# Moving GpSimd's stream sums and the first gating products into the convolution of a language-model tower

## The chip, the cores and the metric

The kernel runs on one core of a Trainium2 chip: TensorE (PE) for products and turns, VectorE (DVE), ScalarE (ACT) and GpSimd (POOL) for elementwise work, SyncE (SP) for most transfers. The metric is the device time of one execution in microseconds. One more execution was recorded by the hardware profiler, and its times are those of the rows below.

## The reference, cut to what matters

Four streams (b = 0 to 3) of 1024 tokens go through a tower of an embedding, four blocks with residual sums, 64 features wide. The change touches the first block only, a gated long convolution in place of attention:

```
h = take(W.T, x)                                  # embedding, masked where x == 0
xn = layernorm(h)
u = silu(xn @ u_w.T + u_b);  v = silu(xn @ v_w.T + v_b)      # 192 wide
y = irfft(rfft(v, 2n) * rfft(a, 2n))[:n]          # a: kernel of a small position network
out = (u * y) @ o_w.T + o_b
x_r = silu(srms((xn - out) @ t_w.T + t_b))
h = h + xn + x_r                                  # the block gives xn + x_r, h is the residual
xn2 = layernorm(h)                                # what the next block reads
```

After it come a product-key memory block, an attention block and a mixture of experts, which this text calls the mixer.

## The kernel before, in words

The program is four blocks one after the other, each with one hand-written list of instructions for each engine; all engines meet at a barrier between blocks: `embed_stage`, `conv_stage`, `gate_stage`, `mixer_stage`. Order within an engine is that of its list, and semaphores say what waits for what. The tensors st_h, tz_xn, tz_u, tz_v and tz_y hold h, xn, u, v and y of all four streams, 128 tokens to a row of partitions, 8 such rows to a stream.

`conv_stage` transforms v by products with a table, multiplies by the kernel's spectrum on VectorE (`product`), and transforms back: 64 products on TensorE (L576), each pair copied out by ScalarE (L598). The back transform runs in two halves: half 0 holds streams 0 and 1, half 1 streams 2 and 3. VectorE's `gather_waves(half)` sums the 16 waves of a half into tz_y. All its operands lie in SBUF.

`gate_stage` goes through the streams in a pipeline. VectorE multiplies u and y of stream 0 (L967), GpSimd those of streams 1 to 3 (`gate_rows`, L792), and GpSimd adds xn to h for each stream between them (`add_rows`, L796). On TensorE, `turn(b)` transposes u*y (16 products, L816 and L817), `project(b)` multiplies by o_w (L826, L827), `weigh(b)` by t_w (L835), `flip(b)` transposes the new xn. On ScalarE, `copy_gated(b)` copies the turned product out of PSUM (L870, L871), then `square`, `root`, `silu`, `deviation` and `copy_rows` follow. On VectorE, four memsets set the rows of ones and zeros that carry the biases (L968 to L971, semaphore ones_set), then `differ(b)` takes xn - out (L928), `mean` and `divide` normalise, `norm_a(b)` adds to h and begins the layer norm (L952 to L955), `norm_b(b)` ends it. TensorE waits for the weights and for the ones ahead of the first turn. The identity that the transposes use is loaded once in the embedding and once more in the gate.

## Time and profile before

| | us |
|---|---|
| median of 3 runs | 3322.91 (3321.53 to 3324.5) |
| the profiled execution: time | 3329.95 |
| its span | 3328.1 |
| embedding | 0 to 91 |
| convolution | 91 to 209 |
| gate | 209 to 290.6 |
| mixer | 290.6 to 3328.1 |

Over the whole span TensorE is busy 84% and VectorE 82%, but that is an average over stages. The rows of the sections below are of three kinds. A timeline row gives when an instruction (or a run of like ones) starts, how long it takes, its engine and line, and in brackets how long the engine had been idle and what released it. A table row gives a stretch and how long each engine was busy in it, with the granted TensorE clock (1.00 is 2.4 GHz, 0.50 is 1.2 GHz). An fp32 product shows as two passes in a row's count.

### The profile page before, as it was taken

What the parts mean: (1) busy time and instruction counts of PE and PEld (TensorE: products, weight loads), DVE (VectorE), ACT (ScalarE), POOL (GpSimd) and SP (SyncE); (2) the same over time, 40 slices, a digit from 0 to 9 for tenths busy, and PEclk for the clock granted to TensorE, in tenths of its full rate; (3) what the DMA queues carried; (4) which work ended last, traced back from release to release, by engine and by line L of the source; (5) the groups of instructions that cost most, each with busy time, mean ns of one, the idle gap of its engine ahead of it and who ended that gap; (6) DMA issues with size and microseconds to landing.
All of it is one profiled execution on the core that took longest, in us unless ns stands there. A gap on an engine that the chain in (4) does not pass through costs nothing. (4 is left out here: it accounts for less than half of the span.)

```text
span 3328.1 us, 39343 instructions
## 1 busy us (share of the span) xinstructions
PE 2803.7 (84%) x9750; PEld 1333.8 (40%) x9750; DVE 2745.1 (82%) x10000; ACT 2051.7 (62%) x4514; POOL 2049.2 (62%) x2094
## 2 busy tenths in 40 slices
PE   4863466888989898989897989999988889899988
PEld 2431222343434343434344434344444434444433
DVE  8666987989898989897889998997989898966423
ACT  4222455676767676767686767676686767676422
POOL 4010577777777777777666777776657777776200
PEclk8975677999999999999898989999999899999989
DMA  1001122222222222222121222221212222221000
GB/s 43 26 10 49 34 65 63 64 64 61 67 64 65 63 64 65 63 64 63 49 67 41 70 61 70 56 73 50 66 47 62 65 65 63 64 63 49 20 0 4
DMA packets 85770, 179.92 MB, mean 54 GB/s; under 512 B 40193, under 2 KB 41251, under 8 KB 85542
## 3 DMA queue, kind: packets, MB, share of 16 engines
q0 software_dynamic: 66560, 135.40, 16.0%
q1 hardware_dynamic: 18982, 42.01, 4.0%
q8 instruction: 79, 1.29, 0.2%
q14 instruction: 149, 1.22, 0.1%
HBM read 176.22 MB, written 1.05 MB: 53 GB/s over the span
## 5 line engine op out<-in xcount | busy, mean ns | idle before, releaser
L1333 POOL DMA_INDIRECT mx_G<-in_kv_table,mx_slot_i x2048 | 1993.1, 973 | 815.4 <-issue 606.4
L1361 PE MATMUL mx_acc<-mx_W,mx_table 128*128 128x512 f32 x2048 | 1114.1, 626 | 0.3 <-ACT mx_kvT L1562 0.3
L1719 DVE SCALAR_TENSOR_TENSOR mx_W<-mx_D,mx_W 128x512 f32<-128x512 f32 x1024 | 697.2, 681 | 260.6 <-ACT mx_W L1555 258.5
L1623 ACT ACTIVATE mx_GT<-mx_G,mx_slot_w 128x128 f32<-128x128 f32 x2048 | 759.0, 494 | 208.9 <-DMA mx_G<-in_kv_table,mx_slot_i 208.5
L1555 ACT ACTIVATE mx_W<-mx_D 128x512 f32<-128x512 f32 x1024 | 606.9, 593 | 165.1 <-PE mx_D L1351 160.7
L1361 PEld LDWEIGHTS mx_acc<-mx_W,mx_table 128*128 128x128 f32 x2048 | 412.6, 203 | 193.8 <-issue 114.8
L1351 PE MATMUL mx_D<-mx_U,mx_pick_b 96*128 96x512 bf16 x1024 | 412.3, 403 | 60.0 <-DVE mx_W L1719 58.4
L1579 ACT ACTIVATE mx_PT<-mx_area 128x512 f32<-128x512 f32 x480 | 246.8, 514 | 284.9 <-PE mx_area L1411 147.0
L1373 PE MATMUL mx_O<-mx_PT,mx_KVs 128*65 128x512 f32 (+3 forms) x768 | 312.7, 489 | 16.9 <-ACT mx_OT L1571 8.7
L1387 PE MATMUL mx_area<-mx_KTa,mx_QTa 64*128 64x512 f32 (+3 forms) x384 | 179.3, 548 | 156.7 <-DVE mx_mx_part L1954 126.2
L1936 DVE TENSOR_REDUCE mx_KVs<-mx_GT 128x128 f32<-128x2048 f32 x128 | 291.8, 2280 | 6.9 <-ACT mx_GT L1623 6.7
L1351 PEld LDWEIGHTS mx_D<-mx_U,mx_pick_b 96*128 96x128 bf16 x1024 | 106.4, 104 | 270.1 <-issue 133.1
L1373 PEld LDWEIGHTS mx_O<-mx_PT,mx_KVs 128*65 128x65 f32 x768 | 101.7, 137 | 216.2 <-issue 171.3
L1387 PE MATMUL mx_area<-mx_KTb,mx_QTb 64*128 64x512 f32 (+3 forms) x384 | 183.1, 559 | 0.0
L1387 PEld LDWEIGHTS mx_area<-mx_KTa,mx_QTa 64*128 64x128 f32 x384 | 59.6, 194 | 303.7 <-DVE mx_mx_part L1954 194.9
L1407 PE MATMUL mx_area<-mx_QTa,mx_KTa 65*128 65x512 f32 (+3 forms) x384 | 158.6, 494 | 3.2 <-DVE mx_mx_part L1954 2.9
L1407 PE MATMUL mx_area<-mx_QTb,mx_KTb 128*128 128x512 f32 (+3 forms) x384 | 156.2, 488 | 0.0
L1954 DVE TENSOR_REDUCE mx_mx_part<-mx_area 128x2 f32<-128x1024 f32 (+3 forms) x128 | 130.1, 1016 | 12.5 <-PE mx_area L1387 6.9
L1636 ACT ACTIVATE mx_hot<-mx_FI 128x864 uint16<-128x864 uint32 x128 | 116.7, 913 | 23.1 <-DVE mx_row L1889 23.1
L1458 PE MATMUL mx_X<-st_keys,mx_qpk 128*128 128x256 f32 x256 | 76.0, 423 | 43.0 <-ACT mx_S L1591 20.3
L792 POOL TENSOR_TENSOR tz_u<-tz_u,tz_y 128x1536 f32<-128x1536 f32 x3 | 11.8, 3950 | 160.4 <-POOLq L460 160.4
L1407 PEld LDWEIGHTS mx_area<-mx_QTa,mx_KTa 65*128 65x128 f32 x384 | 71.6, 192 | 86.2 <-issue 65.3
(380 smaller groups left out, 4370.6 us busy)
## 6 DMA issues: line engine op xcount, KB each, us to landing
mx_table<-in_kv_dense SPq DMA_DIRECT2D x64, 512.0 KB, 3.7
mx_G<-in_kv_table,mx_slot_i POOLq DMA_INDIRECT x2048
tz_table<-in_c_dft SPq DMA_DIRECT2D x1, 2048.0 KB
tz_table<-in_c_idft SPq DMA_DIRECT2D x8, 256.0 KB, 2.6
out_h<-mx_xc SPq DMA_DIRECT2D x4, 256.0 KB, 3.8
mx_G<-in_c_pick SPq DMA_DIRECT2D x1, 528.0 KB
st_h<-in_tok_W,em_ids POOLq DMA_INDIRECT x32, 2.5
st_keys<-in_pk_keys SPq DMA_DIRECT2D x1, 512.0 KB, 3.9
```

The source lines that it names most:

```text
L1333: pool.indirect_dma_start(G[g % RING][:, r, :], None, a["kv_table"], bass.IndirectOffsetOnAxis(slot_i[n % 2][:, k, r:r + 1], 0))\
L1351: pe.matmul(D_ps[c % 3][:, :], pick_b[:, step, :], U[n % 2][:, ih, cols], start=False, stop=True, skip_group_check=True).then_inc(d_ready, 1)
L1361: pe.matmul(acc[:, :], table[:, tile, :], W[c % TILE_RING][:, :], start=(tile == 0), stop=(tile == TILES - 1)).then_inc(applied, 1)
L1373: pe.matmul(O_ps[0:D + 1, first:HALF], values, PT[k % 4][:, first:HALF], start=(kb == 0), stop=last, skip_group_check=True).then_inc(weigh ...
L1387: last = pe.matmul(area[indices[x] % 2][:, 0:w], QT[x][lanes[x], qb * P:qb * P + P], KT[x][lanes[x], kh * HALF:kh * HALF + w], start=True, ...
L1407: last = pe.matmul(bank[:, first:HALF], KT[x][:, kb * P:kb * P + P], QT[x][:, group * HALF + first:(group + 1) * HALF], start=True, stop=n ...
L1555: act.activation(W[c % TILE_RING][:, :], D_ps[c % 3][:, :], ACT.Exp).then_inc(p_done, 1)
L1579: act.activation(PT[k % 4][:, first:HALF], area[index % 2][:, first:HALF], ACT.Gelu if use[0] == "HID" else ACT.Exp).then_inc(prob_ready, 1)
L1623: last = act.activation(GT[:, :, i], G[g % RING][:, i, :], ACT.Copy, scale=slot_w[n % 2][:, k, i:i + 1])
L1719: dve.scalar_tensor_tensor(W[c % TILE_RING][:, :], D_ps[c % 3][:, :], 0.0, W[c % TILE_RING][:, :], ALU.is_ge, ALU.mult).then_inc(w_done, 1)
L1936: dve.tensor_reduce(both, rows, AX, ALU.add).then_inc(kv_ready, 1)
L1954: dve.tensor_reduce(dst, banks[:, :, 0:w], AX, ALU.max).then_inc(scores_taken, 2)
```

## The change

The identity is kept from the embedding (st["ident"]), so the gate loads it no more. In the convolution GpSimd gets a list of its own: the four additions of xn to h at once, then, after a new semaphore half_done, which VectorE raises between the two gatherings, the products u*y of streams 0 and 1. It waits for its own work at the end. TensorE gets 16 products behind the last of the back transform, whose result nobody reads. In the gate, VectorE's product for stream 0 and GpSimd's for stream 1 and its additions are gone; the first turn comes ahead of the waits for the weights and the ones, and turns 0 and 1 wait for no product. ScalarE copies stream 2 before the silus of streams 0 and 1. VectorE takes `norm_a(0)` ahead of `differ(2)` and `norm_a(1)` ahead of `differ(3)`.

```diff
@@ -202,7 +202,7 @@
         m = Mem(nc, ctx, "em")
         ids = m.sb("ids", [P, TB], I32)
         not_pad = m.sb("not_pad", [P, TB])
-        ident = m.sb("ident", [P, P])
+        ident = st["ident"]
         uv_w = m.sb("uv_w", [P, 2 * D1])
         rpe_w = m.sb("rpe_w", [P, 2 * RPE + LAYERS * (RPE * RPE + RPE)])
         pos = m.sb("pos", [P, 2 * NB])
@@ -488,6 +488,8 @@
         product_done = m.sem("product_done")
         wave_ready = m.sem("wave_ready")
         wave_copied = m.sem("wave_copied")
+        half_done = m.sem("half_done")
+        rows_done = m.sem("rows_done")
         block = ctx.enter_context(nc.Block())
 
         def columns(r, i, half):
@@ -513,6 +515,17 @@
                 sp.wait_ge(v_ready, 2 * g + 2)
                 sp.wait_ge(spec8_ready, 1 + g // (FB // 2))
                 sp.dma_start(table[:, g, :], a["c_idft"][g * P:(g + 1) * P, :]).then_inc(idft_in[g], 16)
+
+        @block.gpsimd
+        def _(pool):
+            for b in range(B):
+                h = st["h"][:, b * NB:(b + 1) * NB, :]
+                pool.tensor_tensor(h, h, st["xn"][:, b * NB:(b + 1) * NB, :], ALU.add).then_inc(rows_done, 1)
+            pool.wait_ge(half_done, 1)
+            for b in range(B // 2):
+                u = st["u"][:, b * NB:(b + 1) * NB, :]
+                pool.tensor_tensor(u, u, st["y"][:, :, b * D1:(b + 1) * D1], ALU.mult).then_inc(rows_done, 1)
+            pool.wait_ge(rows_done, B + B // 2)
 
         @block.tensor
         def _(pe):
@@ -577,6 +590,8 @@
                                              out_f[:, 2 * g + j, half * HALF:(half + 1) * HALF],
                                              start=(j == 0), stop=(j == 1))
                         last.then_inc(wave_ready, 1)
+            for _ in range(16):
+                pe.matmul(ker_ps[:, 0, 0:HALF], table[:, 0, 0:P], out_f[:, 0, HALF:2 * HALF], start=True, stop=True)
 
         @block.scalar
         def _(act):
@@ -714,8 +729,10 @@
             dve.sem_inc(spec_ready, 1)
             for g in range(FB):
                 product(g)
-            for half in range(2):
-                gather_waves(half)
+            gather_waves(0)
+            chain.wait()
+            dve.sem_inc(half_done, 1)
+            gather_waves(1)
             chain.clear()
 
 
@@ -724,7 +741,7 @@
 
     with ExitStack() as ctx:
         m = Mem(nc, ctx, "gt")
-        ident = m.sb("ident", [P, P])
+        ident = st["ident"]
         o_w1 = m.sb("o_w1", [P, D])
         o_w2 = m.sb("o_w2", [P, D])
         t_w = m.sb("t_w", [P, D])
@@ -747,9 +764,7 @@
         loaded = m.sem("loaded")
         ones_set = m.sem("ones_set")
         dve_steps = m.sem("dve_steps")
-        uy_first = m.sem("uy_first")
         uy_ready = m.sem("uy_ready")
-        h_ready = m.sem("h_ready")
         uyT_ready = m.sem("uyT_ready")
         uyT_copied = m.sem("uyT_copied")
         outT_ready = m.sem("outT_ready")
@@ -776,7 +791,6 @@
 
         @block.sync
         def _(sp):
-            sp.dma_start(ident[:, :], a["c_ident"]).then_inc(loaded, 16)
             sp.dma_start(o_w1[:, :], a["o_w"][0:P, :]).then_inc(loaded, 16)
             sp.dma_start(o_w2[:, :], a["o_w"][P:2 * P, :]).then_inc(loaded, 16)
             sp.dma_start(t_w[:, :], a["t_w"]).then_inc(loaded, 16)
@@ -791,26 +805,16 @@
                 u = st["u"][:, blocks(b), :]
                 pool.tensor_tensor(u, u, y_of(b), ALU.mult).then_inc(uy_ready, 1)
 
-            def add_rows(b):
-                h = st["h"][:, blocks(b), :]
-                pool.tensor_tensor(h, h, st["xn"][:, blocks(b), :], ALU.add).then_inc(h_ready, 1)
-
-            gate_rows(1)
-            add_rows(0)
             gate_rows(2)
-            add_rows(1)
             gate_rows(3)
-            add_rows(2)
-            add_rows(3)
 
         @block.tensor
         def _(pe):
 
             def turn(b):
-                if b == 0:
-                    pe.wait_ge(uy_first, 1)
-                else:
-                    pe.wait_ge(uy_ready, b)
+                if b >= 2:
+                    pe.wait_ge(uy_ready, b - 1)
+                if b:
                     pe.wait_ge(uyT_copied, 2 * b)
                 for t in range(NB):
                     pe.transpose(uyT1_ps[:, t * P:(t + 1) * P], st["u"][:, b * NB + t, 0:P], ident[:, :])
@@ -842,9 +846,9 @@
                     pe.wait_ge(xnT_copied, b - 1)
                 flip_rows(pe, flip_ps[b % 2], xn[:, b % 2], ident).then_inc(xnT_ready, 1)
 
-            pe.wait_ge(loaded, 64)
+            turn(0)
+            pe.wait_ge(loaded, 48)
             pe.wait_ge(ones_set, 2)
-            turn(0)
             project(0)
             turn(1)
             weigh(0)
@@ -898,9 +902,9 @@
             square(1)
             root(0)
             root(1)
+            copy_gated(2)
             silu(0)
             silu(1)
-            copy_gated(2)
             copy_gated(3)
             deviation(0)
             deviation(1)
@@ -945,7 +949,6 @@
 
             def norm_a(b):
                 h = st["h"][:, blocks(b), :]
-                dve.wait_ge(h_ready, b + 1)
                 dve.wait_ge(xr_ready, b + 1)
                 if b >= 2:
                     dve.wait_ge(xn_ready, b - 1)
@@ -963,8 +966,6 @@
                    .then_inc(xn_ready, 1)
 
             summed = []
-            u = st["u"][:, blocks(0), :]
-            dve.tensor_tensor(u, u, y_of(0), ALU.mult).then_inc(uy_first, 1)
             chain.mark(dve.memset(uyT2[D:P, :], 0.0))
             chain.link(dve.memset(dT[D:P, :, :], 0.0))
             dve.memset(uyT2[D:D + 1, :], 1.0).then_inc(ones_set, 1)
@@ -975,10 +976,10 @@
             mean(1)
             divide(0)
             divide(1)
+            norm_a(0)
             differ(2)
-            norm_a(0)
+            norm_a(1)
             differ(3)
-            norm_a(1)
             norm_b(0)
             norm_b(1)
             mean(2)
@@ -2103,6 +2104,7 @@
             st["rpe"] = mt.sb("rpe", [P, NB, 2, RPE])
             st["rpe_split"] = mt.sb("rpe_split", [P, 16, 2 * RPE])
             st["table"] = mt.sb("table", [P, FB, 4 * P])
+            st["ident"] = mt.sb("ident", [P, P])
             st["dft_in"] = mt.sem("dft_in")
             embed_stage(nc, a, st)
             if stages == 1: return probe(nc, m, st)
```

GpSimd's list, from the convolution's (before: the gate's) start to the mixer; tz_u<-tz_u,tz_y is the product u*y, st_h<-st_h,tz_xn an addition, ISA a configuration instruction. Before:

```order
L787 UNCONDITIONAL_BRANCH [waits barrier_Pool_Activation_PE_DVE_SP_gather]
L792 ISA
L792 TENSOR_TENSOR tz_u<-tz_u,tz_y 128x1536
L796 TENSOR_TENSOR st_h<-st_h,tz_xn 128x512
L792 TENSOR_TENSOR tz_u<-tz_u,tz_y 128x1536
L796 TENSOR_TENSOR st_h<-st_h,tz_xn 128x512
L792 TENSOR_TENSOR tz_u<-tz_u,tz_y 128x1536
L796 TENSOR_TENSOR st_h<-st_h,tz_xn 128x512 x2
L725 UNCONDITIONAL_BRANCH
```

After:

```order
L519 UNCONDITIONAL_BRANCH [waits barrier_Pool_Activation_PE_DVE_SP_gather]
L523 ISA
L523 TENSOR_TENSOR st_h<-st_h,tz_xn 128x512 x4
L527 TENSOR_TENSOR tz_u<-tz_u,tz_y 128x1536 [waits cv_half_done]
L527 TENSOR_TENSOR tz_u<-tz_u,tz_y 128x1536
L460 UNCONDITIONAL_BRANCH [waits cv_rows_done]
L801 UNCONDITIONAL_BRANCH [waits barrier_Pool_Activation_PE_DVE_SP_gather]
L806 TENSOR_TENSOR tz_u<-tz_u,tz_y 128x1536 x2
L742 UNCONDITIONAL_BRANCH
```

The additions and two of the products now stand ahead of the barrier at the gate's entry, the products behind cv_half_done.

ScalarE's list from the squares of streams 0 and 1 on; gt_zz is the squares, gt_rms the roots, gt_zn the silus, gt_uyT the turned product. Before:

```order
L877 ACTIVATE gt_zz<-gt_z_ps 128x512 [waits gt_z_ready] x2
L881 ACT_TABLE_LOAD
L881 ACTIVATE gt_rms<-gt_rms 128x8 [waits gt_mean_ready] x2
L885 ACT_TABLE_LOAD
L885 ACTIVATE gt_zn<-gt_zn 128x512 [waits gt_zn_ready] x2
L870 ACTIVATE gt_uyT<-gt_uyT_ps 128x1024 [waits gt_outT_ready,gt_uyT_ready]
L871 ACTIVATE gt_uyT<-gt_uyT_ps 64x1024
L870 ACTIVATE gt_uyT<-gt_uyT_ps 128x1024 [waits gt_outT_ready,gt_uyT_ready]
L871 ACTIVATE gt_uyT<-gt_uyT_ps 64x1024
```

After:

```order
L881 ACTIVATE gt_zz<-gt_z_ps 128x512 [waits gt_z_ready] x2
L885 ACT_TABLE_LOAD
L885 ACTIVATE gt_rms<-gt_rms 128x8 [waits gt_mean_ready] x2
L874 ACTIVATE gt_uyT<-gt_uyT_ps 128x1024 [waits gt_outT_ready,gt_uyT_ready]
L875 ACTIVATE gt_uyT<-gt_uyT_ps 64x1024
L889 ACT_TABLE_LOAD
L889 ACTIVATE gt_zn<-gt_zn 128x512 [waits gt_zn_ready] x2
L874 ACTIVATE gt_uyT<-gt_uyT_ps 128x1024 [waits gt_outT_ready,gt_uyT_ready]
L875 ACTIVATE gt_uyT<-gt_uyT_ps 64x1024
```

The copies of stream 2 moved from behind the silus to behind the roots.

VectorE's list in the gate from the last scaling of stream 1 on; gt_dT<-st_xnT,gt_outT_ps is `differ`, st_h<-st_h,gt_zn to the COPY is `norm_a`. Before:

```order
L943 TENSOR_TENSOR gt_zn<-gt_z_ps,gt_rms 128x512 [waits gt_dve_steps]
L928 TENSOR_TENSOR gt_dT<-st_xnT,gt_outT_ps 64x1024 [waits gt_z_ready,gt_outT_ready]
L952 TENSOR_TENSOR st_h<-st_h,gt_zn 128x512 [waits gt_xr_ready,gt_h_ready]
L178 TENSOR_REDUCE gt_stat<-st_h 128x8 [waits gt_dve_steps]
L179 TENSOR_SCALAR gt_stat<-gt_stat 128x8 [waits gt_dve_steps]
L180 TENSOR_TENSOR gt_xc<-st_h,gt_stat 128x512 [waits gt_dve_steps]
L181 TENSOR_TENSOR gt_sq<-gt_xc 128x512 [waits gt_dve_steps]
L182 TENSOR_REDUCE gt_stat<-gt_sq 128x8 [waits gt_dve_steps]
L183 TENSOR_SCALAR gt_stat<-gt_stat 128x8 [waits gt_dve_steps]
L955 COPY gt_stat<-gt_stat 128x8 [waits gt_dve_steps]
L928 TENSOR_TENSOR gt_dT<-st_xnT,gt_outT_ps 64x1024 [waits gt_z_ready,gt_outT_ready]
L952 TENSOR_TENSOR st_h<-st_h,gt_zn 128x512 [waits gt_xr_ready,gt_h_ready]
```

After:

```order
L947 TENSOR_TENSOR gt_zn<-gt_z_ps,gt_rms 128x512 [waits gt_dve_steps]
L955 TENSOR_TENSOR st_h<-st_h,gt_zn 128x512 [waits gt_xr_ready]
L178 TENSOR_REDUCE gt_stat<-st_h 128x8 [waits gt_dve_steps]
L179 TENSOR_SCALAR gt_stat<-gt_stat 128x8 [waits gt_dve_steps]
L180 TENSOR_TENSOR gt_xc<-st_h,gt_stat 128x512 [waits gt_dve_steps]
L181 TENSOR_TENSOR gt_sq<-gt_xc 128x512 [waits gt_dve_steps]
L182 TENSOR_REDUCE gt_stat<-gt_sq 128x8 [waits gt_dve_steps]
L183 TENSOR_SCALAR gt_stat<-gt_stat 128x8 [waits gt_dve_steps]
L958 COPY gt_stat<-gt_stat 128x8 [waits gt_dve_steps]
L932 TENSOR_TENSOR gt_dT<-st_xnT,gt_outT_ps 64x1024 [waits gt_z_ready,gt_outT_ready]
L955 TENSOR_TENSOR st_h<-st_h,gt_zn 128x512 [waits gt_xr_ready]
L178 TENSOR_REDUCE gt_stat<-st_h 128x8 [waits gt_dve_steps]
```

The difference of stream 2, which projection 3 and weights 2 wait for, moved behind the whole of `norm_a(0)`.

## Rows read from the trace of the kernel before

**Rows 1.** Stage table: stretch, length, busy time (instructions) by engine, clock, DMA
```profile
209.00:290.60 81.60, 45.94 (x196) 26.20 (x196) 37.93 (x69) 23.99 (x33) 16.63 (x7) 0.69 0.04 11
```

**Rows 2.** Timeline of the convolution: start, duration, engine, instruction [idle before]
```profile
100.80 0.74 DVE L615 TENSOR_SCALAR cv_spec<-cv_spec_ps,cv_sign 16x512 f32<-16x512 f32 x1 [9.76 <-PE cv_spec_ps L525]
...
154.23 41.55 PE L576 MATMUL cv_v_ps<-cv_out_f,tz_table 128*128 128x384 f32 x128
...
191.18 0.96 DVE L608 TENSOR_TENSOR tz_y<-cv_out_f 128x768 f32<-128x768 f32 x1 [0.42 <-ACT cv_out_f L598]
...
196.34 0.96 DVE L608 TENSOR_TENSOR cv_out_f<-cv_out_f 128x768 f32<-128x768 f32 x1 [0.27 <-ACT cv_out_f L598]
```

**Rows 3.** Busy table of VectorE in the convolution's second gathering
```profile
188.10:208.70 20.60, 19.66 (x36) 0.75 0.00 0
```

**Rows 4.** Timeline of the gate's start
```profile
209.02 1.76 DVE L967 TENSOR_TENSOR tz_u<-tz_u,tz_y 128x1536 f32<-128x1536 f32 x1 [0.42 <-PEq L460]
...
209.09 4.98 POOL L792 TENSOR_TENSOR tz_u<-tz_u,tz_y 128x1536 f32<-128x1536 f32 x1 [160.44 <-POOLq L460]
...
211.05 0.91 DVE L968 MEMSET gt_uyT<- 64x1024 f32 x1 [0.27 <-issue]
...
214.02 1.27 POOL L796 TENSOR_TENSOR st_h<-st_h,tz_xn 128x512 f32<-128x512 f32 x1
...
215.24 3.43 POOL L792 TENSOR_TENSOR tz_u<-tz_u,tz_y 128x1536 f32<-128x1536 f32 x1
...
215.66 1.76 DVE L971 MEMSET gt_dT<- 1x2048 f32 x1 [0.38 <-issue]
...
217.53 0.45 PE L816 MATMUL gt_uyT_ps<-gt_ident,tz_u 128*128 128x128 f32 x1 [21.75 <-DVE gt_dT L971]
...
219.84 3.44 POOL L792 TENSOR_TENSOR tz_u<-tz_u,tz_y 128x1536 f32<-128x1536 f32 x1
...
223.19 1.97 PE L826 MATMUL gt_outT_ps<-gt_uyT,gt_o_w 128*64 128x512 f32 x2 [2.02 <-ACT gt_uyT L871]
```

**Rows 5.** Clock table: stretch, length, TensorE busy, granted clock
```profile
195.80:198.40 2.60, 0.00 (x0) 0.99 0.00 0
...
198.40:209.00 10.60, 0.00 (x0) 0.50 0.00 0
...
242.40:246.00 3.60, 0.00 (x0) 1.00 0.00 0
```

**Rows 6.** Timeline of the gate's middle and the mixer's first product
```profile
242.87 1.28 ACT L885 ACT_TABLE_LOAD   x1
...
245.53 1.01 ACT L870 ACTIVATE gt_uyT<-gt_uyT_ps 128x1024 f32<-128x1024 f32 x1
...
247.49 1.97 PE L826 MATMUL gt_outT_ps<-gt_uyT,gt_o_w 128*64 128x512 f32 x2 [5.14 <-ACT gt_uyT L871]
...
253.86 1.21 DVE L928 TENSOR_TENSOR gt_dT<-st_xnT,gt_outT_ps 64x1024 f32<-64x1024 f32 x1 [8.91 <-PE gt_outT_ps L827]
...
255.00 0.68 DVE L952 TENSOR_TENSOR st_h<-st_h,gt_zn 128x512 f32<-128x512 f32 x1
...
257.74 1.07 PE L826 MATMUL gt_outT_ps<-gt_uyT,gt_o_w 128*64 128x512 f32 x2 [0.28 <-ACT gt_uyT L871]
...
259.02 0.17 DVE L955 COPY gt_stat<-gt_stat 128x8 f32<-128x8 f32 x1
...
261.42 1.21 DVE L928 TENSOR_TENSOR gt_dT<-st_xnT,gt_outT_ps 64x1024 f32<-64x1024 f32 x1 [2.23 <-PE gt_outT_ps L827]
...
262.69 2.00 PE L835 MATMUL gt_z_ps<-gt_t_w,gt_dT 128*128 128x64 f32 x16 [1.31 <-DVE gt_dT L928]
...
267.72 0.66 PE L189 MATMUL gt_uyT_ps<-gt_ident,gt_xn 128*64 128x128 f32 x2 [3.04 <-DVE gt_xn L962]
...
273.23 0.29 ACT L881 ACTIVATE gt_rms<-gt_rms 128x8 f32<-128x8 f32 x2
...
290.71 2.04 PE L1454 MATMUL mx_X<-st_xnT,st_pk_w 64*128 64x512 f32 x2 [1.36 <-PEq L725]
```

## The prediction

> **What bounds the kernel now.** I read the views in this order. The stage table first: the gate, from 209.0 to 290.6 us, keeps no engine busy for more than 46 of its 81.6 us [rows 1], so it is a chain of hand-overs, and a microsecond taken from that chain moves all that follows; the mixer's first product starts when the gate ends. Of the other 3037 us the change touches nothing. Second, the timeline of the convolution's end: TensorE is done at 154.23 + 41.55 = 195.8 us, and VectorE alone works on until 208.6, 0.42 us before the gate [rows 2, 4]. Third, the timeline of the gate's start: the first turn begins at 217.53 after 21.75 us of idle TensorE, and what released it is VectorE's last memset, not the product that it turns [rows 4]. Fourth, the clock table [rows 5], and fifth the rows of the gate's middle [rows 6].
>
> **The adds of the streams.** Four GpSimd adds of 1.27 us [rows 4] move to the start of the convolution. They need only what the embedding left, 5.1 us in all, and VectorE idles 9.76 us there, up to its first instruction at 100.80 [rows 2]; TensorE is not concerned. Cost nothing; in the gate they stood behind the products, which nobody was late for, so the gain there is nothing either. If that cover were gone (GpSimd slow to start), they would still have 90 us until GpSimd's next work.
>
> **The two products in the convolution.** This is the price of the change. GpSimd is released at about 188 us, when the first half is gathered, and needs two products of 3.43 us. From 188.1 to 208.7 VectorE is busy 19.66 us [rows 3], nearly all of it instructions with two inputs in SBUF. Do the two engines run side by side? Before has one such meeting: GpSimd's first product, begun at 209.09 beside VectorE's own product of 1.76 us (209.02 to 210.78), took 4.98 us, the other two 3.43 and 3.44. The excess, 1.54 us, is about the overlap, 1.69 us: GpSimd did not move while VectorE worked. Memsets don't do that: the 3.43 us product of 215.24 ran beside the memset of 215.66 at the length of the one that had no company [rows 4]. The other reading of the 1.54 us is GpSimd's own start, since a configuration instruction (ISA in the order) stands right before it; so the bounds are 0 (they run freely) and 6.9 us (fully one after the other). I take the upper, as the overlap fits it. VectorE's two idle pieces in the half, 0.42 and 0.27 us [rows 2], absorb some: 6.86 - 0.69 = 6.2 us. Whether VectorE waits for GpSimd or GpSimd for VectorE and the barrier for GpSimd gives the same end. The gate starts at 209.0 + 6.2 = 215.2. The wait and increment added between the halves cost VectorE about 0.1 us, within the 0.42.
>
> The Trainium skill speaks against the change here. Its page "SBUF — State Buffer", section "Who interferes with whom", says that a VectorE instruction with two SBUF inputs contends with a GpSimd instruction that reads SBUF, and that whoever comes first holds the port for its whole instruction while the other fully blocks; memsets with no input don't contend. By that rule the term is the upper bound, 6.2 us, and the trace's 1.54 us agrees; without the rule and with the other reading of that row it would be 0.
>
> **The idle products.** A product of the inverse transform takes 41.55 us / 64 = 0.65 us (two passes each in the row's count of 128) [rows 2], so 16 take 10.4 us and end at 206.2. TensorE was idle there; they write a bank that nobody reads, so their direct cost is nothing, with VectorE's tail as cover. Do they keep the clock? It stayed at full (2.4 GHz) for about 2.6 us after TensorE stopped at 195.8 and for at least 3.6 us after 242.4; after 195.8 it then went to half (1.2 GHz) [rows 5]. With the gate at 215.2 the gap is 9 us: the first turn runs at half clock as before. Were the gate to start at 209.0, the gap would be 2.8 us and the turn might run at full clock, but the turn isn't what is late, as the next paragraph shows: gain nothing either way.
>
> **The start of the gate.** Before, the first projection began 223.19 - 209.02 = 14.2 us after VectorE's first instruction [rows 4]. Now the turn starts with the gate (3.6 us at half clock: 217.53 to 223.19, less 2.02 idle), ScalarE's two copies take 2.0 (245.53 to 247.49 [rows 6]), together 5.7 with the hand-overs. What is late next is the memsets, since the projection still waits for the ones: 211.05 to 217.42 are 6.4 us, and the product ahead of them is gone. So it begins 6.5 us after the gate's start: 7.7 us less. The three weight loads, issued within 1.3 us and landing in about 2 each, are in time; the identity needs no load. The projection itself stays at half clock.
>
> **ScalarE's and VectorE's order.** Up to the roots of streams 0 and 1 everything keeps its distances. I keep before's times here and add the shifts later. The copies of stream 2 start after the roots at 242.87 instead of 245.53 and end 1.9 us later, so projection 2 starts at 244.8, 2.5 us after turn 2 left off instead of 5.1 [rows 6]; the clock need not have fallen by then [rows 5], and it takes 3.6 us (257.74 to 261.4) instead of 6.4 (247.49 to 253.86) [rows 6]: done at 248.4. The silus come behind the copies: the table load of 1.28 and half of the 1.4 us that two silus took (244.15 to 245.53), so stream 0's is done at 246.8. VectorE now takes stream 0's norm first, 4.2 us (255.00 to 259.19): until 251.0. So the difference of stream 2 starts at 251.0, not at 248.5, and ends at 252.2 (before 255.07). Weights 2 take just under 2.0, projection 3 starts at 254.0 (257.74) and ends at 257.6; norm 1 fits between (252.2 to 256.3). Difference 3 at 257.7 (261.42), weights 3 at 258.9 (262.69), done at 260.7. Before, the flips came only at 267.72, behind norm 1 and the first scaling on VectorE [rows 6]. That scaling is the 1.0 us from norm 1's end (261.42 + 1.2 + 4.2 = 266.8) to 267.72. Now norm 1 is over when difference 3 ends at 258.9 and the scaling is done at 259.9, so the flips follow the weights at once: 267.72 - 260.7 = 7.0 us earlier. Being joined to work at full clock they may also run at full: two flips of 2.3 us (267.72 to 273.23 less a hand-over and the 1.0 us copy) would save about 2 us together. Bounds of this term: 7.0 - 1.2 = 5.8 (the clock falls before projection 2, of which the norm hides most) and 9.0; I take 8.0. From the roots of 273.23 on the order is the old one.
>
> **Sum.** +6.2 - 7.7 - 8.0 = -9.5 us, against the profiled execution 3329.95 - 9.5 = 3320.4 (span 3328.1 to 3318.6). That execution lies 7 us above the median of the runs, 3322.91, for reasons that leave the difference alone; on the median the forecast is 3313.4 us. A difference below 0.2%, 6.6 us, can't be told from none here.
>
> **Rivals.**
> A, no blocking: GpSimd's excess was its own start, and the products cost VectorE nothing. Then the gate starts at 209.0 and the sum is -15.7: 3307.2. For it: the configuration instruction; against it: the match of 1.54 with 1.69.
> B, slower: the port is handed over piece by piece, so that VectorE's whole second half goes at half its pace and GpSimd's products stretch along it. At most it doubles the 19.66 us, +20 instead of +6.2, against -15.7 elsewhere: +4.3, 3327.2. It turns from faster to slower when the half grows by more than 15.7 us. For it: nothing in the trace shows who yields how often; against it: VectorE's product of 209.02 kept a normal length beside GpSimd, and only 6.9 us of GpSimd work exist to wait for.
> C, the clock: turn 0 and projection 0 are now parted by 2.8 us and follow a gap; if the clock doesn't rise in projection 0, turn 1 (+1.8), projection 1 (+2.8), turn 2 (+1.8) and projection 3 (+2.8) run at half clock: +9, together about -0.5: 3322.4. Against it: before had 2.0 us in that place and the clock was full from turn 1 on.
>
> **How the numbers follow.** Forecast 0.64 (its own range 3310 to 3317), A 0.20, C 0.10, B 0.06. The range takes in A and most of the way to C: 3305.5 to 3320. Faster by over 0.2%: 0.57 of the forecast and A, 0.77. Same: 0.07 of the forecast, C, and 0.02 of B, 0.19. Slower: 0.04.
>
> **What would show it.** In the profile after: GpSimd's two products between 188 and 215 us, at least one longer than 3.43 us, or VectorE gaps of about 3.4 us; the gate's first turn at about 215 (A: 209; B: over 225). The first projection 6.5 us behind the gate's start, released by a memset. The clock full from turn 1 to the first flips, half in turn 0. From the gate's first instruction to the mixer's first product 66 us (before 290.71 - 209.02 = 81.7 [rows 4, 6]). I am wrong if that stretch is not under 70 us, or if the convolution ends within 2 us of its old time or more than 10 us after it.

## The result and the profile after

The changed kernel takes 3312.4 us (median of 13 runs, 3310.5 to 3315.8) where before takes 3323.7 in the same group of runs. The ratio is 0.9965 with a 95% interval of 0.9957 to 0.9974, that is 11.6 us less (8.6 to 14.3). The forecast was -9.5 us. The profiled executions lie further apart, spans of 3310.6 and 3328.1 us, of which 12.9 us arise in convolution and gate and 1.3 in the embedding, which the change doesn't touch; the other 3.3 us lie in the mixer, which the change doesn't touch either and whose length goes from 3032.7 to 3037.8 us over the profiles of all kernels here but the second group's (below). One timed execution each of the kernels f2 (9688 us) and a2 (9453 us), further below, stands far from all others and is in no ratio.

I measure stages between instructions that every version has: "convolution" from its first transfer (before 91.50, after 90.25) to the gate's first transfer (208.98, 212.99), "gate" from there to the mixer's first product.

| term | forecast | before | after | difference |
|---|---|---|---|---|
| convolution | +6.2 | 117.5 | 122.7 | +5.3 |
| gate's start to first projection | -7.7 | 14.2 | 6.8 | -7.5 |
| first projection to second turn | 0 | 6.5 | 5.2 | -1.2 |
| second turn to the roots of stream 2 | -8.0 | 43.6 | 34.7 | -8.8 |
| roots to the mixer's first product | 0 | 17.5 | 16.8 | -0.7 |
| sum | -9.5 | 199.2 | 186.3 | -12.9 |

The convolution's second half after, which answers to [rows 2, 3] (timeline: start, duration, engine, line, operands, count, [idle before <- releaser]):

```profile
186.22 3.43 POOL L527 TENSOR_TENSOR tz_u<-tz_u,tz_y 128x1536 f32<-128x1536 f32 x1 [90.96 <-DVEq L734]
186.24 3.83 DVE L623 TENSOR_TENSOR tz_y<-cv_out_f 128x384 f32<-128x384 f32 x1
...
189.61 3.76 POOL L527 TENSOR_TENSOR tz_u<-tz_u,tz_y 128x1536 f32<-128x1536 f32 x1
189.99 3.79 DVE L626 TENSOR_TENSOR tz_y<-cv_out_f 128x384 f32<-128x384 f32 x1
...
193.75 10.48 PE L594 MATMUL cv_ker_ps<-cv_out_f,tz_table 128*128 128x384 f32 x32
...
212.06 0.55 DVE L626 TENSOR_TENSOR tz_y<-cv_out_f 128x384 f32<-128x384 f32 x1
...
213.03 0.45 PE L820 MATMUL gt_uyT_ps<-tz_ident,tz_u 128*128 128x128 f32 x1 [8.80 <-PEq L460]
```

Two VectorE instructions of 384 columns, 0.55 us each before, take 3.83 and 3.79. GpSimd's first product started at 186.22, VectorE's instruction at 186.24; GpSimd's ended at 189.65, VectorE's 0.42 us later. GpSimd's second product, from 189.61, took 3.76 us instead of 3.43, so it stood still for the 0.33 us in which VectorE finished; VectorE's next, from 189.99, ended 0.41 us after that product. The two engines take turns, one instruction each, and it is VectorE, with the shorter instructions, that loses most. The wait shows as a longer instruction and not as a gap ahead of it. The two grew by 3.28 + 3.24 = 6.5 us; 0.69 of it filled VectorE's earlier idle pieces [rows 2].

The gate's start, which answers to [rows 4]:

```profile
216.63 1.02 ACT L874 ACTIVATE gt_uyT<-gt_uyT_ps 128x1024 f32<-128x1024 f32 x1 [22.19 <-PE gt_uyT_ps L821]
...
217.88 1.76 DVE L972 MEMSET gt_dT<- 1x2048 f32 x1 [0.38 <-issue]
...
219.75 1.90 PE L830 MATMUL gt_outT_ps<-gt_uyT,gt_o_w 128*64 128x512 f32 x2 [3.16 <-DVE gt_dT L972]
```

TensorE's first turn began at 213.03, right at the barrier, was copied out by 218.6 (217.55 + 1.00, the second copy not shown), and the projection then waited for the last memset (217.88 + 1.76), as the [3.16 <-DVE gt_dT L972] on PE's row says. The middle of the gate, which answers to [rows 6]:

```profile
238.09 1.00 ACT L874 ACTIVATE gt_uyT<-gt_uyT_ps 128x1024 f32<-128x1024 f32 x1
...
240.05 1.79 PE L830 MATMUL gt_outT_ps<-gt_uyT,gt_o_w 128*64 128x512 f32 x2 [2.37 <-ACT gt_uyT L875]
...
241.97 0.69 DVE L955 TENSOR_TENSOR st_h<-st_h,gt_zn 128x512 f32<-128x512 f32 x1 [1.68 <-ACT gt_zn L889]
...
246.08 1.21 DVE L932 TENSOR_TENSOR gt_dT<-st_xnT,gt_outT_ps 64x1024 f32<-64x1024 f32 x1
...
249.31 1.07 PE L830 MATMUL gt_outT_ps<-gt_uyT,gt_o_w 128*64 128x512 f32 x2
...
252.99 1.21 DVE L932 TENSOR_TENSOR gt_dT<-st_xnT,gt_outT_ps 64x1024 f32<-64x1024 f32 x1 [1.59 <-PE gt_outT_ps L831]
...
254.26 2.00 PE L839 MATMUL gt_z_ps<-gt_t_w,gt_dT 128*128 128x64 f32 x16 [1.31 <-DVE gt_dT L932]
...
256.19 0.43 PE L189 MATMUL gt_uyT_ps<-tz_ident,gt_xn 128*64 128x128 f32 x2
...
259.71 0.29 ACT L885 ACTIVATE gt_rms<-gt_rms 128x8 f32<-128x8 f32 x2
```

The norm of stream 0 (from 241.97) ends where the difference of stream 2 begins, 246.08; after the weights of stream 3 (254.26) the flips come with no gap (256.19, their idle bracket is empty), where before TensorE had waited 3.04 us. The clock, which answers to [rows 5] (stretch, length, TensorE busy, granted clock, DMA):

```profile
204.30:209.00 4.70, 0.00 (x0) 1.00 0.00 0
209.00:213.00 4.00, 0.00 (x0) 0.57 0.00 0
213.00:216.30 3.30, 3.27 (x16) 0.50 0.36 78
216.30:219.75 3.45, 0.29 (x3) 0.99 0.39 144
219.75:223.16 3.41, 3.41 (x5) 0.51 0.02 5
240.05:245.30 5.25, 5.25 (x8) 0.67 0.00 0
253.00:259.00 6.00, 4.49 (x34) 1.00 0.00 0
```

The clock rose while TensorE waited ahead of the first projection, fell again as the projection began, and rose again 3.4 us into it, at 223.2. In before it rose 5.9 us into the projection:

```profile
223.19:229.00 5.81, 5.81 (x7) 0.50 0.01 3
```

### The profile page after: what moved, and what is told of

Its sections match the earlier page's. It is cut to its first block and busy times, and to the rows that moved or that the text cites. A ratio compares the mean times of both kernels' runs of the same rounds, so it can differ in the third digit from the quotient of the medians.

```text
span 3310.6 us, 39405 instructions
## 1 busy us (share of the span) xinstructions
PE 2803.2 (85%) x9782; PEld 1331.7 (40%) x9782; DVE 2749.2 (83%) x9999; ACT 2053.1 (62%) x4514; POOL 2047.8 (62%) x2095
## 5 line engine op out<-in xcount | busy, mean ns | idle before, releaser
L1741 DVE MATCH_REPLACE8 mx_S<-mx_V,mx_S 128x64 f32<-128x64 f32 x512 | 103.9, 207 | 0.0
```

## The experiments

Stage lengths of all of them, in us, from one profile each; the ratio is to before, from 5 to 13 timed runs of each kernel, with its 95% interval. Stages that no edit concerned differ between profiles by up to 1.5 us (the changed kernel's convolution: 122.7, 122.8 and 123.2, and 124.2 in e2).

| kernel | convolution | start to 1st projection | it to 2nd turn | 2nd turn to roots | gate | conv. + gate | ratio |
|---|---|---|---|---|---|---|---|
| before | 117.5 | 14.2 | 6.5 | 43.6 | 81.7 | 199.2 | 1 |
| changed | 122.7 | 6.8 | 5.2 | 34.7 | 63.5 | 186.3 | 0.9965 (0.9957 to 0.9974) |
| e1 products in the gate | 117.4 | 11.8 | 6.0 | 34.7 | 69.7 | 187.1 | 0.996 (0.9947 to 0.9974) |
| e2 no idle products | 124.2 | 6.8 | 5.9 | 34.7 | 64.5 | 188.7 | 0.996 (0.9946 to 0.9974) |
| e3 old orders | 122.5 | 6.8 | 5.1 | 42.9 | 72.2 | 194.6 | 0.9985 (0.9975 to 0.9994) |
| e6 only the turn first | 117.4 | 8.6 | 5.9 | 43.3 | 75.2 | 192.6 | 0.9983 (0.9974 to 0.9992) |
| e4 writes only | 116.9 | 6.8 | 6.5 | 38.0 | 68.7 | 185.6 | one run |
| e5 eight pieces | 123.0 | 6.8 | 5.3 | 34.7 | 64.0 | 186.9 | one run |
| a1 changed (second group) | 122.8 | 6.8 | 5.3 | 34.7 | 63.6 | 186.4 | 0.9957 (0.9935 to 0.998) |
| f1 VectorE first (second group) | 116.5 | 8.6 | 5.2 | 34.7 | 65.5 | 182.0 | 0.9981 (0.9952 to 1.001) |
| f2 memsets on GpSimd (second group) | 116.7 | 7.3 | 3.6 | 34.7 | 62.4 | 179.1 | 0.9967 (0.9942 to 0.9993) |
| f3 clock kept (second group) | 116.7 | 5.9 | 3.6 | 36.3 | 63.2 | 179.9 | 0.9969 (0.9943 to 0.9996) |
| f4 best | 116.9 | 5.9 | 3.6 | 36.0 | 62.6 | 179.4 | 0.994 (0.9927 to 0.9953) |
| a2 changed | 123.2 | 6.8 | 5.2 | 34.7 | 63.8 | 187.0 | 0.996 (0.9947 to 0.9973) |

The kernels marked "second group" were timed together at a time when before takes 3934.8 us. The changed kernel's convolution and gate are the same there (186.4 us against 186.3), the mixer is longer (3636.5 us in a1's profile against 3034.1), the embedding too (the convolution starts at 106.8 us and not 90.3), and the mixer scatters by tens, so those ratios, with intervals of 9 to 11 us either way, resolve no such difference and I read that group's stages alone.

### e1, products back in the gate

```diff
 conv, gpsimd:
-            pool.wait_ge(half_done, 1)
-            for b in range(B // 2): ... u * y ...
 conv, vector, between the two gatherings:
-            chain.wait()
-            dve.sem_inc(half_done, 1)
 gate, gpsimd:
+            gate_rows(1)
 gate, tensor, in turn(0):
+                    pe.wait_ge(uy_first, 1)
 gate, vector, ahead of the memsets:
+            dve.tensor_tensor(u, u, y_of(0), ALU.mult).then_inc(uy_first, 1)
```

> The changed kernel, but the products of streams 0 and 1 are back in the gate (stream 0 on VectorE ahead of its memsets, stream 1 on GpSimd); the additions stay in the convolution, the first turn ahead of the waits for weights and ones. Theory (GpSimd and VectorE exclude each other while both read SBUF): from the convolution's first transfer to the gate's first instruction falls from 122.8 us (changed kernel) back to 117.5 us, no VectorE instruction of 384 columns takes over 0.6 us; the first projection comes 8.5 to 9 us after the gate's start instead of 6.7. Net 3 to 4 us faster than the changed kernel, ratio to before about 0.9955. Rival (the 5.3 us of the convolution come from the added wait and increment or from the idle products): the stretch stays at about 122 us and the kernel is 2 us slower than the changed one.

The convolution fell back to 117.4 us, as the theory said. The edit takes out the wait and the increment between the halves too, so it clears the idle products and the additions, which stayed, but not that pair; e4 below keeps the pair and has no longer convolution either, so the products are what lengthened it. The rest missed: convolution and gate came out at 187.1 us, not 3 to 4 below the changed kernel. The timeline at the gate's start shows why:

```profile
209.18 3.42 POOL L801 TENSOR_TENSOR tz_u<-tz_u,tz_y 128x1536 f32<-128x1536 f32 x1 [112.42 <-POOLq L460]
209.20 5.01 DVE L968 TENSOR_TENSOR tz_u<-tz_u,tz_y 128x1536 f32<-128x1536 f32 x1 [0.42 <-PEq L460]
...
212.56 4.96 POOL L801 TENSOR_TENSOR tz_u<-tz_u,tz_y 128x1536 f32<-128x1536 f32 x1
```

Before, VectorE had started 0.07 us ahead (209.02 against 209.09 [rows 4]), its product took 1.76 and GpSimd's 4.98. Here GpSimd is 0.02 us ahead, takes 3.42, and VectorE's takes 5.01 = 3.3 + 1.7. The same pair, the other order, the other loser; and GpSimd's next product, begun at 212.56, waited in its turn until VectorE's ended at 214.21, and took 4.96. What turned the order round is in the lists: in before, as in e6, GpSimd's configuration instruction stands right ahead of its first product in the gate, which began 0.11 us after the gate's first transfer in both; in e1 it stands in the convolution, and the product began 0.03 us after it. VectorE began 0.04 to 0.05 us after it in all three. The prediction's other reading of the 1.54 us, a start-up of GpSimd's own after its configuration instruction, falls too. In the changed kernel that instruction stands ahead of the convolution's four additions, and these took 4.91 us, no more than four times the 1.27 of before. That the additions cost nothing, as predicted, shows in e1, which has them at the same place and a convolution of 117.4 us against before's 117.5. The row is of the changed kernel:

```profile
90.35 4.91 POOL L523 TENSOR_TENSOR st_h<-st_h,tz_xn 128x512 f32<-128x512 f32 x4 [41.42 <-POOLq L201]
```

And in e6, with VectorE first as before, GpSimd's product took 4.99 again.

### e2, no idle products

```diff
-            for _ in range(16):
-                pe.matmul(ker_ps[:, 0, 0:HALF], table[:, 0, 0:P], out_f[:, 0, HALF:2 * HALF], start=True, stop=True)
```

> The changed kernel without the 16 products behind the back transform. Theory (they buy next to nothing, because the clock is at half again when the turn begins, or soon after): the first turn takes 3.6 us as in the changed kernel, the first projection starts at the same distance from the gate's start (6.7 us, set by the memsets); the clock may rise up to 1.3 us later in the first projection, since it lasted 5.2 us in the changed kernel and 6.5 in before. Time within 1.5 us of the changed kernel, ratio to before about 0.9967. Rival (they are what shortens the gate): projection and the turns after it at half clock, 4 us or more slower than the changed kernel, ratio 0.9978 or more.

The theory holds as far as the runs can tell: turn at half clock, the projection at the same distance, and the stretch from it to the second turn 0.7 us longer. Of the 2.4 us by which convolution and gate exceed the changed kernel's, 1.4 lie ahead of VectorE's second half (97.4 us against 96.0), where no idle product stands yet. The ratios are the same within their intervals. Stage of the turn, and the projection:

```profile
214.60:221.30 6.70, 3.65 (x16) 0.50 0.37 113
221.30:227.30 6.00, 5.94 (x9) 0.60 0.01 3
```

### e3, old orders

```diff
-            copy_gated(2)
             silu(0)
             silu(1)
+            copy_gated(2)
 and on VectorE:
-            norm_a(0)
             differ(2)
-            norm_a(1)
+            norm_a(0)
             differ(3)
+            norm_a(1)
```

> The changed kernel with ScalarE's and VectorE's orders of before in the gate (copies of stream 2 behind the silus of streams 0 and 1, difference of stream 2 and 3 ahead of the norms of streams 0 and 1). Theory: the stretch from the second turn's start to the roots of stream 2 goes from 34.7 us back to before's 43.6, the ratio to before rises to 0.999 (some 9 us slower than the changed kernel). Rival (the order matters little, and the stretch shrank by the earlier start and the clock): the stretch stays under 38 us and the kernel within 4 us of the changed one.

Hit: 42.9 us from the second turn to the roots, 8.1 more than the changed kernel, and the ratio at 0.9985. The two orders together are worth 8 of the 12.9 us; no run takes back one of them alone, so how it splits between the copies and the norms isn't shown. With them TensorE waits as long as before for the copies of stream 2, and for VectorE ahead of the flips:

```profile
242.57 1.97 PE L830 MATMUL gt_outT_ps<-gt_uyT,gt_o_w 128*64 128x512 f32 x2 [5.14 <-ACT gt_uyT L875]
...
255.83 1.21 DVE L932 TENSOR_TENSOR gt_dT<-st_xnT,gt_outT_ps 64x1024 f32<-64x1024 f32 x1 [2.23 <-PE gt_outT_ps L831]
...
262.12 0.66 PE L189 MATMUL gt_uyT_ps<-tz_ident,gt_xn 128*64 128x128 f32 x2 [3.02 <-DVE gt_xn L965]
```

### e6, only the first turn moved

```diff
-            pe.wait_ge(loaded, 64)
+            turn(0)
+            pe.wait_ge(loaded, 48)
             pe.wait_ge(ones_set, 2)
-            turn(0)
```

> The kernel of before with two edits: the identity is kept from the embedding, and the first turn comes ahead of TensorE's waits for the weights and the ones. Products, additions, orders as in before, no idle products. Theory (most of the gate's earlier start comes from this one line, since the memsets and the turn then run side by side): the first projection starts 8.5 to 9 us after the gate's start (before 14.2), everything else as before, 5.5 us faster, ratio 0.9983. Rival (the product moved to GpSimd is what is needed): under 2 us faster, ratio over 0.9993.

Hit: first projection 8.6 us after the gate's start, ratio 0.9983. Of the 7.5 us that the changed kernel gains at this place, 5.7 come from where the turn stands in TensorE's list, and 1.8 from the product ahead of the memsets, for which the convolution pays 5.3. So moving the products costs about 3.5 us more than it gives; the gain of the change comes from the turn and the orders.

### e4, GpSimd only writes

```diff
-            for b in range(B // 2): ... u * y ...
+            for b in range(7):
+                pool.memset(st["keys"][:, :, :], 0.0).then_inc(rows_done, 1)
+                pool.wait_ge(rows_done, B + 1 + b)
```

> The changed kernel, in which GpSimd, at the place of the two products, clears a 128x1024 tile seven times (it only writes, some 7 us in all); u of streams 0 and 1 is therefore not multiplied by y. Theory (what excludes the engines is the reading of SBUF by both): no VectorE instruction grows, all of 384 columns stay at 0.55 us, and the stretch from the convolution's first transfer to the gate's first instruction is 117.5 to 118 us. Rival (any GpSimd work on SBUF stops VectorE): VectorE instructions of over 1 us, and the stretch at 121 us or more.

Hit (the stretch a little under its range): 116.9 us, and VectorE's instructions keep their length beside 6.7 us of memsets (seven of 0.95):

```profile
186.43 7.00 POOL L526 MEMSET st_keys<- 128x1024 f32 x7 [90.98 <-DVEq L733]
...
186.46 0.56 DVE L622 TENSOR_TENSOR tz_y<-cv_out_f 128x384 f32<-128x384 f32 x1
186.94 0.55 DVE L625 TENSOR_TENSOR tz_y<-cv_out_f 128x384 f32<-128x384 f32 x1
187.41 0.95 DVE L622 TENSOR_TENSOR tz_y<-cv_out_f 128x768 f32<-128x768 f32 x1
```

Against the changed kernel's 122.7 this prices the two products in the convolution at 5.8 us in one profile each. The gate of this execution was 5.2 us longer than the changed kernel's though its lists are the same. 1.3 of it are the first projection, which ran at half clock for longer (6.5 us to the second turn); 3.3 lie behind the second turn: there the third projection ran at full clock and ended early, TensorE then stood 1.76 us behind the norm, and the products by t_w (2.82 us instead of 2.00) and the fourth projection ran at half clock. f3 shows the same.

### e5, the products in eight pieces

```diff
-                u = st["u"][:, b * NB:(b + 1) * NB, :]
-                pool.tensor_tensor(u, u, st["y"][:, :, b * D1:(b + 1) * D1], ALU.mult).then_inc(rows_done, 1)
-            pool.wait_ge(rows_done, B + B // 2)
+                for t in range(0, NB, 2):
+                    u = st["u"][:, b * NB + t:b * NB + t + 2, :]
+                    pool.tensor_tensor(u, u, st["y"][:, t:t + 2, b * D1:(b + 1) * D1], ALU.mult).then_inc(rows_done, 1)
+            pool.wait_ge(rows_done, B + 4 * (B // 2))
```

> The changed kernel with each of GpSimd's two products cut into four (128x384 each, same result). Theory (exclusion for the length of one instruction, the engines taking turns): up to eight VectorE instructions grow, each by about one piece (0.85 to 1.0 us), none to over 2 us, GpSimd's pieces spread over twice the time, and the sum of VectorE's growth stays 6.5 to 8 us, so the convolution's stretch is 122.5 to 124 us. Rival (VectorE is starved until GpSimd's queue is empty): one or two VectorE instructions of over 3 us and the rest unchanged.

The theory's picture, with growths a little under its range: eight VectorE instructions grew, by 0.67 to 0.85 each (0.85 to 1.0 expected) (0.55 to 1.40 and 1.35, 0.96 to 1.74, 1.63, ...), 6.2 us in all (6.5 to 8 expected), and the convolution took 123.0 us. GpSimd's first piece, which went first, took 1.0 us, the other seven 1.3 to 1.7 each, and VectorE's instructions stand between them. The engines take turns, one instruction each; cutting the work finer changes who waits how often, not how long in total.

```profile
187.72 1.40 DVE L624 TENSOR_TENSOR tz_y<-cv_out_f 128x384 f32<-128x384 f32 x1
189.05 1.35 DVE L627 TENSOR_TENSOR tz_y<-cv_out_f 128x384 f32<-128x384 f32 x1
190.32 1.74 DVE L624 TENSOR_TENSOR tz_y<-cv_out_f 128x768 f32<-128x768 f32 x1
```

### a1, f1, f2, f3: towards a version without the price

```diff
 f1, on top of e1 (GpSimd's list in the gate):
+            pool.wait_ge(uy_first, 1)
             gate_rows(1)
 f2, on top of e1: the four memsets leave VectorE for GpSimd, ahead of gate_rows(1);
     weigh(0), not project(0), waits for the second pair
 f3, on top of f2:
-            for _ in range(16):
+            for _ in range(20):
+            filler(2)
             turn(0)
+            filler(3)
 ...
             turn(2)
+            filler(3)
             project(2)
 where filler(n) is n products of 384 columns into outT_ps, which project overwrites
```

> The changed kernel once more, as the measure for the three beside it. Every theory expects ratio 0.9965 to before, 122.7 us from the convolution's first transfer to the gate's start and 6.7 us from there to the first projection.

> The changed kernel with both products back in the gate, and GpSimd's first one waiting for VectorE's. Theory (the engine whose two-input instruction starts first holds the other off for its length): VectorE's product takes 1.76 us instead of the 5.0 us that it took when GpSimd had started 0.02 us ahead of it, GpSimd's three take 3.4 us each, the convolution's stretch is 117.4 us, the first projection comes 8.6 us after the gate's start: convolution and gate together 3 to 4 us shorter than in the changed kernel, ratio 0.9955. Rival (the 5.0 us was VectorE's late start, not GpSimd): 5 us again.

f1 hit, its gain a little above the expected 3 to 4 us: with GpSimd held until VectorE's product is over, that product takes 1.76 us and GpSimd's 3.44, and convolution and gate are 4.4 us shorter than a1's.

```profile
222.16 1.76 DVE L969 TENSOR_TENSOR tz_u<-tz_u,tz_y 128x1536 f32<-128x1536 f32 x1 [0.42 <-PEq L460]
...
223.99 3.44 POOL L801 TENSOR_TENSOR tz_u<-tz_u,tz_y 128x1536 f32<-128x1536 f32 x1 [113.34 <-DVE tz_u L969]
```

> As the kernel with the products in the gate, but the four memsets run on GpSimd beside VectorE's product and ahead of GpSimd's products. Theory (writes alone don't exclude): VectorE's product 1.76 us beside a memset, the first projection 7.6 us after the gate's start, set by the turn and its copies and no longer by the ones; 4 to 5 us shorter than the changed kernel, ratio 0.9952. Rival (GpSimd's memsets hold VectorE too): VectorE's product over 2.5 us.

f2: the mechanism hit, the size missed to the good side, 7.3 us shorter. Beside the memset VectorE's product keeps 1.76 us, and the projection is now released by ScalarE's copy:

```profile
222.58 0.95 POOL L804 MEMSET gt_uyT<- 64x1024 f32 x1 [111.71 <-POOLq L460]
222.62 1.76 DVE L978 TENSOR_TENSOR tz_u<-tz_u,tz_y 128x1536 f32<-128x1536 f32 x1 [0.42 <-PEq L460]
```

Most of the surplus is the clock: from the first projection to the second turn it is 3.6 us in this execution, 5.2 in a1.

> As the one before, with 20 idle products behind the back transform instead of 16, and 2, 3 and 3 more ahead of the first turn, behind it and behind the third turn (stream 2). Theory (the clock falls where TensorE stands still): first turn at full clock in 1.8 us, first projection 3.5 us instead of 5.2 to 6.5, third projection 3.5 instead of 5.2; another 4 to 6 us shorter, ratio 0.994. Rival (idle products don't hold the clock, or delay the turns by as much as they give): within 1.5 us of the one before.

f3 missed. The clock did stay at full through turn and first projection, 1.4 us earlier at the second turn. But the third projection at full clock only ended earlier, the difference of stream 2 stood behind the norm of stream 0 as before, TensorE idled 1.76 us, and the fourth projection began at half clock (1.97 us for its first pair instead of 1.07). What the first part gave (1.4 us), the second took (1.6), and with a tail 0.6 us longer f3 came out 0.8 us behind f2 where 4 to 6 ahead were expected.

```profile
246.70 1.07 PE L842 MATMUL gt_outT_ps<-gt_uyT,gt_o_w 128*64 128x512 f32 x2 [0.28 <-ACT gt_uyT L891]
...
252.74 1.21 DVE L948 TENSOR_TENSOR gt_dT<-st_xnT,gt_outT_ps 64x1024 f32<-64x1024 f32 x1
...
254.01 2.63 PE L851 MATMUL gt_z_ps<-gt_t_w,gt_dT 128*128 128x64 f32 x16 [1.76 <-DVE gt_dT L948]
...
256.56 1.97 PE L842 MATMUL gt_outT_ps<-gt_uyT,gt_o_w 128*64 128x512 f32 x2
```

### f4 and a2: the best version, where before takes 3325.9 us

```diff
             turn(2)
-            filler(3)
             project(2)
```

> Products in the gate, memsets on GpSimd, 20 idle products behind the back transform, 2 ahead of the first turn and 3 behind it, but none behind the third turn. Theory (the third projection is hidden behind the norm of stream 0, so a kept clock there only moves TensorE's gap behind it, where the clock then fell): the stretch from the second turn to the roots of stream 2 is 34.7 us again (36.3 with those three), convolution and gate together 177 to 178.5 us (changed kernel 186.4, before 199.2), so 8 to 9 us faster than the changed kernel and 20 to 21 faster than before, ratio 0.994 where the mixer is undisturbed. Rival (the time that the gate gives is taken back in the mixer): conv and gate as short, but the kernel within 3 us of the changed one.

> The changed kernel once more beside it, as its measure. Every theory expects 186.4 us for convolution and gate together and ratio 0.9965 to before.

f4 runs at 3305.6 us where before takes 3325.9, ratio 0.994 (0.9927 to 0.9953), and the changed kernel beside it 3312.9: about 20 us under before and 7 under the changed kernel, and the rival (taken back in the mixer) falls. Convolution and gate are 179.4 us, 1 to 2 more than expected: the stretch from the second turn to the roots is 36.0 and not 34.7. So f4's theory missed there: without the three idle products behind the third turn the stretch is as long as with them (36.3 in f3). The start is as meant, with everything at full clock:

```profile
207.31 0.95 POOL L804 MEMSET gt_uyT<- 64x1024 f32 x1 [111.84 <-POOLq L460]
...
207.35 1.48 PE L833 MATMUL gt_outT_ps<-tz_xn,tz_ident 128*64 128x384 f32 x4 [0.35 <-PEq L460]
207.35 1.76 DVE L985 TENSOR_TENSOR tz_u<-tz_u,tz_y 128x1536 f32<-128x1536 f32 x1 [0.43 <-PEq L460]
...
213.24 1.04 PE L842 MATMUL gt_outT_ps<-gt_uyT,gt_o_w 128*64 128x512 f32 x2
```

The clock fell later instead, at 227.0, during stream 1's products by t_w and 1.3 us after TensorE's 1.30 us wait for the difference of stream 1, so that turn 2 (from 228.04) ran mostly at half. It rose while TensorE stood behind that turn, and fell again in the third projection:

```profile
217.00:223.00 6.00, 5.72 (x38) 1.00 0.00 0
227.00:230.40 3.40, 3.40 (x19) 0.50 0.00 0
230.40:233.80 3.40, 1.39 (x8) 1.00 0.00 0
233.80:237.20 3.40, 3.40 (x5) 0.51 0.00 0
```

f3's list is the same up to the end of turn 2, and its clock did not fall there. The difference between the two executions came ahead of the edit, so it isn't the edit's.

## Why the prediction was right, point by point

- **The price in the convolution** was the term in doubt, between 0 and 6.9 us; 6.2 was taken, 5.3 came against before and e1, 5.8 against e4, 6.3 for f1 against a1. The mechanism is the one given: e1, e4 and e5 show that the fp32 products of VectorE and GpSimd with both inputs in SBUF go one after the other, that memsets don't hinder them, and that whoever starts first goes first; f1 shows that both keep their length when they don't meet. The prediction left open who would wait; VectorE lost 6.5 us, GpSimd 0.3. "At least one longer than 3.43 us" held by that 0.3 us; the other sign, gaps of VectorE, did not show, because its wait lies inside its instructions. The rule of the Trainium skill, page "SBUF — State Buffer", section "Who interferes with whom", was worth more than the single row it was weighed against: it says that issue order decides who blocks, and e1 against before shows it with 0.02 and 0.07 us of head start.
- **The start of the gate**: forecast 6.5 us to the projection, set by the memsets; 6.8 came, released by the memset as said. The term was -7.7, measured -7.5.
- **The first projection** was taken as unchanged; it was 1.2 us shorter. This is the clock: it rose 3.4 us into the projection in the changed kernel (the rise at 216.3 ahead of it did not last) and 5.9 us into it before. "The projection itself stays at half clock" was so for two thirds of it. The step "gain nothing either way" for the idle products failed by a little at most: e2 without them had 0.7 us more there, and no difference in time that its five runs can tell. Whether the idle products gave the 0.7 us, one profile of each can't say: e4, which has them, took 6.5 us there, as long as before.
- **The orders**: -8.0 forecast, -8.8 came, 8.1 of it taken back by e3. The single times came out too: with its times moved by the 4.8 us by which the roots of stream 0 came earlier, the forecast has the difference of stream 2 at 246.2 (measured 246.08), projection 3 at 249.2 (249.31) and the flips at 255.9 (256.19). Inside it one step failed as put: the third projection was to run at full clock after 2.5 us of idle TensorE (3.6 us); after 2.37 us it ran mostly at half (240.05 to 245.32, granted 0.67). It cost nothing, since the norm of stream 0 ran until 246.1 anyway; f3 and e4 show that a faster one gives nothing. The sign "full from turn 1 to the first flips" so failed for this one projection. The full clock in the flips was forecast and came (0.43 and 0.95 us where before had 0.66 and 1.70).
- **The tail** was taken as unchanged and was 0.7 us shorter; its last flip ran mostly at full clock (1.09 us for seven passes where before took 1.70).
- The forecast of 3313.4 us compares with 3312.4; the difference to before, -9.5, with -11.6 (-14.3 to -8.6). By stages the one profile gives -12.9, 3.4 us beyond the forecast: four terms came out better than forecast, by 0.7 to 1.2 us each, and the start 0.2 worse. So the small errors add up rather than cancel, and that the medians agree within 1 us is in part luck. Rival A (no blocking) and B (VectorE at half its pace for the whole half) fall with the same rows: two instructions grew, and the others kept 0.55 us. C (half clock from turn 1 on) falls by the clock, which rose at 223.2, ahead of turn 1, and stayed at full through turn 2; only the third projection had half clock, and that was hidden.

## What to carry to other kernels

Before moving elementwise work to GpSimd "beside" VectorE, look at the operands of both: where each read its inputs from SBUF (VectorE with two), the time was added and not hidden, and then it must replace more on the critical path than it adds. Here it didn't (5.3 us paid, 1.8 gained); memsets beside such work cost nothing. The gain came from orders that cost nothing: a step that needs nothing placed ahead of the waits (5.7 us), and, together 8 us, a copy that TensorE waits for placed ahead of work that nobody waits for yet, and the norms of the first streams placed into VectorE's wait for the next. Where two engines may collide at a stage's start, say by a semaphore which goes first: f1 did, and lost nothing to the collision.

## What the runs showed of the hardware that I had not expected

- A head start of 0.02 us decides which engine loses 3.3 us (e1). That GpSimd had it there, and VectorE a lead of 0.07 us in before and e6, goes with a configuration instruction that stands ahead of GpSimd's product in these two and not in e1. An instruction this short can so be worth 3 us; that it alone did it is read from three traces, and no run moved it by itself.
- The granted clock stayed at full for 4.7 us and more after TensorE's last idle product in the changed kernel, 2.6 us at the same place before, yet in f4 it fell with no gap of TensorE over 1.30 us since the gate's start. Idle products shortened the half-clock stretches, but up to the roots of stream 2 new ones came elsewhere (f3: one, around the start of the fourth projection; f4: two, at turn 2 and in the third projection), and the same list gave full clock in f3 and half in f4 at turn 2. What exactly decides it these runs leave open.
- In the second group the mixer took about 600 us longer with the same program, while convolution and gate agreed within 0.2 us. The record gives the same chip number for that group and for f4 and a2, where the mixer took 3032.7 us, so a difference between chips isn't shown. The cause stays open; it is why stage lengths, not times, carry the comparison of f1, f2 and f3.
